# A fused perceiver kernel: TensorE order of two batches in four, small exponentials on GpSimd, a convolution in two parts

## What is computed

```python
x = x + xattn(layernorm(x), ctx)    # per batch: 32 queries on 257 context rows, 16 heads of 16
x = x + ssd(layernorm(x))           # per token: softplus(dt), cumulative sums, exp(+-cumA), norm
x = x + moe(layernorm(x))           # 8 experts, top 2, inner width 704

# ssd: proj = xs @ W_in.T; conv_out = sum_k xp[:, k:k+s] * conv_w[:, k] + conv_b   (first batch only)
#      dt = softplus(dt + dt_bias); cumA = cumsum(A_param * dt)
#      norm = exp(cumA) * cumsum(exp(-cumA));  out = (Y[0] / norm) @ W_out.T
# moe: top_w, sel = top_k(logits, 2); top_w = softmax(top_w); out += gate * (silu(x@wg) * (x@wu)) @ wd
```

## Time and profile before

| what | value |
|---|---|
| median of 3 runs | 1404.13 us (1404.12, 1404.13, 1407.59) |
| the profiled execution | 1407.54 us |
| its span, first to last instruction | 1405.7 us |
| busy: TensorE, VectorE, ScalarE, GpSimd | 96%, 75%, 68%, 55% |
| mean granted TensorE clock | 0.989 of full |
| attention stage | 0 to about 897 us |
| pairs, then single tiles | about 906 to 1283 us, then to the end |

### The profile page before, as it was taken

One profiled execution on the slowest core, in us unless ns is written; L12 is line 12 of the kernel. 1 busy time (PEld: TensorE's weight loads), 2 busy tenths in 40 slices (PEclk: granted clock), 3 DMA queues, 4 the chain that ended last, 5 costly groups with the idle time before them and its releaser, 6 DMA issues.

```text
span 1405.7 us, 53222 instructions
## 1 busy us (share of the span) xinstructions
PE 1351.9 (96%) x16566; PEld 1227.3 (87%) x16566; DVE 1053.2 (75%) x4207; ACT 961.4 (68%) x2684; POOL 770.5 (55%) x1355
## 2 busy tenths in 40 slices
PE   6979999999999999999999999999899999998997
PEld 5858888888888888888888888789899899998997
DVE  4637878888888888888888887777677777776774
ACT  4736777777777777777777776566667567666764
POOL 4434665665666566566566655534345455454553
PEclk9989999999999999999999999899999999999998
DMA  6212464455343334334334333156555555555886
GB/s 195 65 38 75 141 190 151 135 191 159 102 120 102 98 111 116 103 94 128 98 101 121 97 91 85 36 163 176 152 146 157 168 177 153 161 175 167 258 258 172
DMA packets 94235, 190.71 MB, mean 136 GB/s; under 512 B 18480, under 2 KB 60976, under 8 KB 88592
## 3 DMA queue, kind: packets, MB, share of 16 engines
q1 hardware_dynamic: 78448, 170.64, 38.4%
q0 software_dynamic: 15680, 18.76, 7.5%
HBM read 158.92 MB, written 31.65 MB: 136 GB/s over the span
## 4 chain that ended last, share of the span: by engine, by line
PE 83%; ACT 5%; DVE 4%; issue 3%; POOL 1%; DMA 1%; ACTq 0%; SPq 0%; DVEq 0%; POOLq 0%; another core or an unknown queue 0%
PE km L609 31%; PE sc L609 22%; PE v_p L609 17%; PE pt L670 5%; PE v_p L670 5%; PE km L692 2%; ACT late_room L1272 2%; DVE late_hidden L1989 2%; DVE late_room L1957 1%; ACT late_hidden L1313 1%; DMA late_rows<-zbuf,gi 1%; PE pt L924 1%; DMA slot_table<-in_pad 0%; ACT L1313 0%; ACT early_room L1127 0%
## 5 line engine op out<-in xcount | busy, mean ns | idle before, releaser
L609 PE MATMUL sc<-late_room 128*128 128x256 f32 (+1 forms) x2578 | 345.6, 289 | 11.7 <-DVE late_hidden L1989 6.0
L609 PEld LDWEIGHTS sc<-late_room 128*128 128x128 f32 x2578 | 325.6, 192 | 17.9 <-issue 9.6
L1151 ACT ACTIVATE early_room<-early_room,nmx 128x257 f32<-128x257 f32 x512 | 255.8, 502 | 50.7 <-DVE nmx L1498 27.4
L1127 ACT ACTIVATE early_room<-v_p 128x512 f32<-128x512 f32 x256 | 152.7, 596 | 149.7 <-PE km L609 127.0
L1498 DVE CUSTOM_DVE_ANT_0 early_room<-sc,early_room 128x257 f32<-128x257 f32 x512 | 193.1, 421 | 69.6 <-PE sc L609 60.9
L2214 POOL TENSOR_TENSOR ctx_lo<-ctx,ctx_hi 128x516 fp32r<-128x516 f32 x128 | 166.6, 1301 | 48.4 <-ACT ctx_hi L1127 48.3
L2343 POOL DMA_INDIRECT out<-late_rows,oi x56 | 94.9, 1695 | 155.4 <-DMA out<-late_rows,oi 111.5
L609 PE MATMUL km<-ctx_hi,wkh 128*128 128x256 f32 x512 | 160.7, 314 | 5.8 <-POOL ctx_lo L2214 5.8
L609 PE MATMUL km<-ctx_lo,wkh 128*128 128x256 f32 x512 | 146.3, 286 | 0.0
L609 PE MATMUL km<-ctx_hi,wkl 128*128 128x256 f32 x512 | 145.6, 284 | 0.0
L609 PE MATMUL v_p<-wvh,ctx_lo 128*128 128x256 f32 x512 | 144.0, 281 | 0.0
(11 more groups left out here) (262 smaller groups left out, 3543.0 us busy)
## 6 DMA issues: line engine op xcount, KB each, us to landing
late_room<-d_split SPq DMA_DIRECT2D x43, 1536.0 KB
ctx<-in_ctx SPq DMA_DIRECT2D x128, 258.0 KB, 2.8
early_room<-in_mask SPq DMA_DIRECT2D x512, 32.1 KB, 1.8
d_split<-pieces SPq DMA_DIRECT2D x24, 512.0 KB
pieces<-in_wd SPq DMA_DIRECT2D x24, 256.0 KB
wg<-in_wg SPq DMA_DIRECT2D x8, 704.0 KB
wu<-in_wu SPq DMA_DIRECT2D x8, 704.0 KB
early_room<-in_x SPq DMA_DIRECT2D x32, 128.0 KB, 2.1
```

What stands on the lines that cost most here:

```text
L609: return nc.tensor.matmul(out, lhsT, rhs, start=start, stop=stop)
L1127: return nc.scalar.activation(out, in_, ACT.Copy, **kw)
L1151: nc.scalar.activation(pr[:, g, :], sm[:, g, :], ACT.Exp, bias=nmx[:, g:g + 1], scale=-1.0, accum_out=rsum[:, g:g + 1]).then_inc(exp_done, 1)
```

## The change

1. TensorE, attention: in batches b = 1 and 3 `scores` moves ahead of both `transpose_probs`. In b = 0 and 2 `project_k` moves ahead of `turn_c`. The softplus scratch moves from the score bank to an SBUF tile, and a wait of `scores` on it goes.
2. GpSimd computes e^x as a power (`euler` ** x) for the last tile's softplus and decays and the last two gates. VectorE copies the sums to SBUF for it (`take_sums`), since they lie in PSUM. ScalarE's exponentials there go.
3. `ssd_conv` is cut after the first two taps; the rest runs behind `split_low` and `last_probs`.
4. Pair stage: VectorE's `ending_b` moves behind the gating of chunks 4 and 5. The end of the small layers moves by one or two pairs. `plan_rest` becomes three pieces of 10, 10 and 9 steps in `ending_a` of pairs 15 to 17.
5. Single tiles: GpSimd gathers tile t+3 in `body(t)` instead of tile t+2.

```diff
@@ TensorE
             def scores(i, b):
-                if b == 1 and runs(i - 2):
-                    pe.wait_ge(a_done, i - 1)
...
             def tile(i):
                 for b in range(TB):
                     nxt, two = following(i, b), following(i, b, 2)
+                    if b in (0, 2) and runs(two[0]):
+                        project_k(*two)
                     turn_c(*((i, b - 1) if b else (i - 1, TB - 1)))
...
+                    if b in (1, 3) and runs(two[0]):
+                        project_k(*two)
                     if runs(two[0]):
-                        project_k(*two)
                         project_v(*two)
                     turn_a(i, b)
                     if runs(i):
                         weigh_values(i, b)
+                    if b in (1, 3) and runs(two[0]):
+                        scores(*two)
                     if runs(nxt[0]):
                         transpose_probs(*nxt, 0)
                     turn_b(i, b)
                     if runs(nxt[0]):
                         transpose_probs(*nxt, 1)
-                    if runs(two[0]):
+                    if b in (0, 2) and runs(two[0]):
                         scores(*two)
...
             def ending_a(p):
+                if p == 7:
+                    pe.wait_ge(lg_done, NT - 1)
+                    sum_a(NT - 1)
+                if p == 9:
+                    pe.wait_ge(sums_done, 2)
+                    sum_decay_and_rank(NT - 1, NT - 2)
...
             def ending_b(p):
-                if p == 6:
-                    pe.wait_ge(lg_done, NT - 1)
-                    sum_a(NT - 1)
-                if p == 7:
-                    sum_decay_and_rank(NT - 1, NT - 2)
...
-                if p == 15:
+                if p == 17:
                     turn_plan(PLAN, False)
@@ ScalarE
             def ending_a(p):
-                if p == 5:
-                    soft_exp(NT - 1)
-                    gate_exp(NT - 2)
-                if p == 7:
-                    decays(NT - 1)
...
-                if p == 11:
-                    gate_exp(NT - 1)
@@ VectorE
             def scratch(j, k):
-                if isinstance(j, int) and j == NT - 1:
-                    return K[:, k * H:(k + 1) * H]
-                return SC[1][:, SP + k * H:SP + (k + 1) * H]
+                return softs[:, k, :]
...
+            def take_sums(j):
+                dve.wait_ge(cum_ready, j + 1)
+                V.tensor_copy(sums[:, 0, :], M[:, 0:H]).then_inc(sums_done, 1)
+                V.tensor_scalar(sums[:, 1, :], M[:, 0:H], -1.0, None, ALU.mult).then_inc(sums_done, 1)
...
             def ending_a(p):
-                if p in (13, 14, 15):
-                    plan_rest(2 * (p - 13) + 1)
+                if p in (15, 16, 17):
+                    plan_rest(p - 15)
             def ending_b(p):
-                if p in (12, 13, 14):
-                    plan_rest(2 * (p - 12))
...
             def body2(p, s):
...
-                ending_b(p)
                 gate_up2(p, 4)
                 gate_up2(p, FULL)
+                ending_b(p)
                 low_h(p, s, 4)
                 low_h(p, s, FULL)
@@ GpSimd
-            def ssd_conv():
+            def ssd_conv(part):
...
+            def powers(dst, x, n, done):
+                G.tensor_tensor(dst, euler[:, 0:n], x, ALU.pow).then_inc(done, 1)
             def tile(i, k=None):
                     if b == 3 and isinstance(i, int) and i == 1:
-                        ssd_conv()
+                        ssd_conv(0)
                     if runs(three[0]):
                         split_low(*three)
...
                         last_probs(*nxt)
+                    if b == 3 and isinstance(i, int) and i == 1:
+                        ssd_conv(1)
             def body2(p, s):
+                if p == 5:
+                    pool.wait_ge(nabs_done, NT)
+                    powers(dtv[:, 2, :], dtv[:, 1, :], H, u_done)
+                if p == 6:
+                    pool.wait_ge(diff_done, NT - 1)
+                    powers(sv[:, 1, 0:1], sv[:, 0, 0:1], 1, gate_e)
+                if p == 8:
+                    pool.wait_ge(sums_done, 2)
+                    powers(dtv[:, 7, :], sums[:, 1, :], H, en_done)
...
                 if p > 0:
                     scatter_pair(p - 1, 1 - s)
                 if p == 8:
+                    powers(dtv[:, 6, :], sums[:, 0, :], H, ep_done)
+                if p == 10:
                     write_slots(NT - 2)
...
             def body(t, s, first=False, last=False):
-                if not first and not last:
-                    gather(t + 2, s)
+                if not last:
+                    gather(t + 3, 1 - s)
```

More of the change, by code:

```diff
@@ L1 @@
+import math
 import concourse.bass as bass
@@ L210, in perceiver @@
         dtv = sb("dtv", [P, 11, H])
+        softs = sb("softs", [P, 4, H])
+        euler, sums = sb("euler", [P, H]), sb("sums", [P, 2, H])
         lg = sb("lg", [P, 4, E])
@@ L594, in _ @@
                     store_z3(NT - 2)
-                if p == 11:
+                if p == 13:
                     store_z3(NT - 1)
-                if p == 15:
+                if p == 16:
                     load_table()
@@ L2062, in ending_b @@
                 if p == 7:
+                    take_sums(NT - 1)
+                if p == 9:
                     norms(NT - 1)
@@ L2065, in ending_b @@
                     scale_y(NT - 1)
-                if p == 8:
+                if p == 10:
                     residual2(NT - 1)
-                if p == 9:
+                if p == 11:
                     normalise3(NT - 1)
-                if p == 10:
+                if p == 12:
                     take_logits(NT - 1)
@@ L2255, in tap @@
                     return taps[:, :, n:n + 1].broadcast_to([P, NC, Q])
-                conv_step(G.tensor_tensor(cv[:, 0], xp[:, :, 0:Q], tap(0), ALU.mult))
-                for n in range(1, KC):
+                if part == 0:
+                    conv_step(G.tensor_tensor(cv[:, 0], xp[:, :, 0:Q], tap(0), ALU.mult))
+                for n in (range(1, 2), range(2, KC))[part]:
                     conv_step(G.tensor_tensor(cv[:, 1], xp[:, :, n:n + Q], tap(n), ALU.mult))
                     conv_step(G.tensor_tensor(cv[:, 0], cv[:, 0], cv[:, 1], ALU.add))
+                if part == 0:
+                    return
                 conv_step(G.tensor_tensor(cT, cv[:, 0], prm("convb").unsqueeze(2).broadcast_to([P, NC, Q]), ALU.add))
@@ L2360, in body2 @@
                     power(2, NT - 2, mv3, var3, rstd3)
-                if p == 9:
+                if p == 5:
[7 more added lines that the diff above has]
+                    powers(dtv[:, 7, :], sums[:, 1, :], H, en_done)
+                if p == 11:
                     power(2, NT - 1, mv3, var3, rstd3)
+                if p == 13:
+                    pool.wait_ge(diff_done, NT)
+                    powers(sv[:, 1, 0:1], sv[:, 0, 0:1], 1, gate_e)
                 if p > 0:
@@ L2400, in _ @@
             pool.wait_ge(con_in, 16)
+            G.memset(euler[:, :], math.e).then_inc(euler_done, 1)
+            pool.wait_ge(euler_done, 1)
             split_low(0, 0)
@@ L2422, in _ @@
             body(2, 0)
-            with pool.Fori(3, NSLOT - 2, 2) as t:
+            with pool.Fori(3, NSLOT - 4, 2) as t:
                 body(t, 1)
                 body(t + 1, 0)
+            body(NSLOT - 4, 1)
+            body(NSLOT - 3, 0, last=True)
             body(NSLOT - 2, 1, last=True)
```

38 lines of the change are left out of this document (17 added, 21 removed).

## The result

| what | before | after |
|---|---|---|
| median of 10 runs each | 1405.63 us (1403.98 to 1408.30) | 1411.62 us (1407.69 to 1416.17) |
| the profiled execution, and its span | 1407.54, 1405.7 us | 1410.20, 1408.4 us |
| ratio of the times, 95% interval | | 1.0042 (1.0030 to 1.0053) |

The account below looks back on a forecast made before the run. TensorE, busy in 96% of the span, was taken as the bound. Terms -6.1 - 0.9 + 3 - 7.9 - 2.1 = -14.0 us gave 1393.5 for the profiled execution; the median was given as 1404.13 - 13 = 1391 us, range 1380 to 1400.

Parts of the forecast that it names:

- the loop's term of the sum: Attention loop: gains and losses net to +0.1 us a tile, times 27 tiles, +3 us (bounds -7 to +9).
- The chain of four ScalarE latencies: Attention loop, b = 3: added-up ScalarE steps have `rp` copied by 420.94, so the keys wait until about 421.04, today's start.
- The rivals: Three alternative outcomes: loop gains, 1381 us, chance 0.2; slow side, 1423 us, 0.06; waits stay, 1398 us, 0.18.
- The slow side: Attention loop: keys wait in both even batches, 1.3 us a tile, +35 us instead of +3, 1423 us; chance 0.06.
- Convolution: Tile 2: `split_low` begins 4.37 us earlier, TensorE idles less and its clock stays up, -6.1 us.
- the low bound of 3.8: Tile 2: the convolution's gain if the clock falls as before, -3.8 us.
- Start: First two tiles: scores fill waits for the copy of the values, 0.45 us each in two places, -0.9 us (0 to -2.3).
- Pair stage: Pair stage: table loads -6.2, `sum_a` -1.1, plan -4.2 and +3.6, together -7.9 us (-4 to -12).
- The term of the table loads: Pair stage: six ScalarE table loads go, 0.5 us of each pair of loads being slack; TensorE gains 6.2 us.
- The plan's pieces: Pair stage: three ten-step VectorE pieces at the pair's start cost about 1.2 us each, +3.6 us.
- the 173 us of the prediction: Pair stage: the thirteen pairs from pair 5's transposes to pair 18's take about 173 us instead of 181.07.
- Single tiles: Single tiles: two waits for gathered rows go because the gather is issued some 4 us earlier, -2.1 us (0 to -2.1).

Follow-up runs that it names:

- loop_back: Changed kernel with TensorE's old order in the attention loop and the softplus scratch back in the score bank: 1394.35 us, ratio 0.9931 to the kernel before.
- back_table_17: loop_back with SyncE's table load one pair later, at pair 17 instead of 16: 1391.98 us, ratio 0.9895 to the kernel before.
- z3_behind: Changed kernel with VectorE's normalisation of z3 behind the keys' copy in b = 2: 1408.70 us, ratio 1.0037 to the kernel before.
- square_behind: Changed kernel with softplus_square behind the second half of the keys' copy on VectorE: 1403.33 us, ratio 0.9988 to the kernel before.

## Why the prediction was wrong

**The failed step** is the last sentence of the part on the loop: "VectorE's scratch in SBUF changes no end, since VectorE has room in each tile." I looked at VectorE's idle time and not at how long an instruction takes that now reads twice from SBUF beside GpSimd. It takes 0.94 us instead of 0.16, stands between the two halves of the keys' copy, and TensorE waits for the second half: 0.27 us a tile by the rows, 0.24 by the edit that takes it away, 0.41 in the old order. That is 6.5 of the 11.7 us by which the loop's term of the sum was missed. Room over a tile is not room at the place.

**Keys and `rp`.** The chain of four ScalarE latencies was right: 1.75 us from the transposes to the keys was forecast, 1.80 measured, with a wait of 0.49. In b = 3 the loss is 0.26 us a tile, most of it because keys, `sum_a` and values take 428.41 - 425.17 = 3.24 us, where keys and values took 3.04. My own figures gave that: 0.01 + 0.14 + 0.08 = 0.23 us. I had booked 0.1 instead. Against it stand the 0.14 us that b = 1 wins, where I took it as even. The two errors cancel, so that the net of 0.12 us for 0.1 was luck.

**Not looked at:** what follows TensorE's product of ynT on VectorE. It ended 1.34 us ahead of the keys and now ends 0.36 ahead; residual, maxima and normalisation come after it and the keys' copy after those. 0.18 us a tile, 4.9 us in all.

Together the loop costs 14.7 us, not 3. The rivals were drawn too narrowly. The slow side had the sign right, but it rested on the keys of b = 1, and there nothing waits in the changed kernel. Most of the loss came from VectorE's late copies of the keys, and for VectorE in the loop the prediction had no rival.

**Convolution.** The keys started 3.5 us earlier, which is the 4.4 of the forecast less the 0.9 us by which tile 2 began late. The clock was the mistake: it fell in spite of the shorter wait, and tile 2 won 3.0 us, under the low bound of 3.8. In loop_back and back_table_17, which are the same program there and keep TensorE's old order, tile 2 took 41.3 and 39.0 us between keys, 4.0 and 6.3 less than before. So a gain of the forecast size can come out, but the middle of my sum counted on it.

**Start.** -0.9 forecast, +0.9 measured. 0.46 is in the first transfer (8.40 for 7.94 us of waiting), which the change does not touch. Tile 1 is 0.5 us longer, and in it the keys wait 0.87 us for `rp`; I had looked only at the waits that the scores would fill.

**Pair stage.** The term of the table loads is right in total, 6.2 forecast and 6.25 by the edit, though not pair by pair. The 0.1 us of idle time that I cited for it stands ahead of the loads, not behind them. The reading holds all the same: in the trace before a load from 986.35 to 987.63 is followed by the exponential at 987.64. The plan's pieces are dearer than forecast: in back_table_17, without the stall, pairs 15 to 17 take 13.52, 14.07 and 14.61 us, 4.9 us over three times 12.43, for 3.6 (small products of TensorE's are in the 4.9 too). What failed is that I moved the writes of slots and the table's load by two and one pairs and priced VectorE's and ScalarE's steps alone: the landing of the scatters was in no term, and it cost the 4.7 us by which the pairs gained 3.2 instead of 7.9. Without the stall, in back_table_17 and in z3_behind, the thirteen pairs take the 173 us of the prediction.

**Single tiles.** -1.5 for -2.1. At the very end 0.3 us comes back: the last scatter waits 2.8 us for the one ahead of it, and no run here shows whether the earlier gathers have to do with it; it stays open.

Of the tests that the prediction named, "wrong if a tile is over 27.4" and "if the pairs do not lose at least 4 us" both hit.

## What to carry to other kernels

When a change moves a small operand from PSUM to SBUF, take each instruction that reads it, look whether its other input is in SBUF, and what GpSimd does at that moment; then ask who waits for the instruction behind it. An order on the busiest engine is only as good as the slowest copy that it shortens the distance to: list for each group how far ahead of its reader it now ends, on all engines, and move the copies with it. Here the kernel lost 9 us in the loop with the scratch's wait gone (a tile of 27.37 us in square_behind), drew level with `rp` ahead of z1T too, and won 11 us once VectorE's heads moved as well (that last step was not tried on the old order).

## What was not expected of the hardware

- A VectorE instruction of 16 columns with two SBUF inputs took 0.94 us beside GpSimd's subtraction of 516 columns, 0.15 to 0.17 us with the same inputs and no such subtraction beside it, and 0.16 us beside one with one input in PSUM. Its end followed GpSimd's by 0.02 to 0.04 us in three kernels, whether it had started 0.38 or 0.78 us behind GpSimd's start.
- The clock at tile 2 is not settled by the program. loop_back and back_table_17 have the same instructions there, wait 0.73 and 0.93 us for the keys, and run at 0.50 and at 1.00 of full clock (1.2 and 2.4 GHz) from 81 to 84 us. In loop_back the mean was 0.76 already from 78 to 81 us, so part of the fall came ahead of that wait. First loop_back, then back_table_17:

```profile
81.00:84.00 3.00, 3.00 (x15) 3.00 (x16) 0.14 (x1) 2.52 (x11) 2.69 (x7) 0.50 0.55 118
```

```profile
81.00:84.00 3.00, 2.10 (x17) 2.10 (x18) 0.56 (x3) 1.44 (x6) 2.77 (x7) 1.00 0.24 44
```

- A scatter of 256 columns landed after 6.8 us with the table's read beside it and the next after 7.7 us with a load of weights beside it, and after 5.2 to 5.9 us in eight later pairs of the same trace. What decides between these is open.
